# One decoder block with routed experts: routing, experts and combine joined in one block of programs

## What is computed

```python
logits = flat @ gate_W.T;  probs = softmax(logits)
top_v, top_i = top_k(probs, 2)                    # 8 experts, 2 for each token
out_e = (silu(x @ w1_e[e]) * (x @ w3_e[e])) @ w2_e[e]      # 128 -> 512 -> 128
routed = sum of top_v * out_e over the token's 2 experts
shared = mean over 8 small shared experts of the same form # together 128 -> 512 -> 128
out = layernorm(x + 0.5 * shared + 0.5 * routed)
```

## Time and profile before

| | us |
|---|---|
| median of 3 runs | 851.56 (851.37 to 851.6) |
| the profiled execution | 843.65 |
| its span | 841.9 |
| TensorE matmul busy | 713.6 (85%) |
| VectorE, ScalarE, GpSimd busy | 487.4, 481.5, 461.6 |
| TensorE's clock, mean | 0.927 of full |

### The profile page before, as it was taken

One profiled execution on the slowest core, in us unless ns is written; L12 is line 12 of the kernel. 1 busy time (PEld: TensorE's weight loads), 2 busy tenths in 40 slices (PEclk: granted clock), 3 DMA queues, 4 the chain that ended last, 5 costly groups with the idle time before them and its releaser, 6 DMA issues.

```text
span 841.9 us, 16996 instructions
## 1 busy us (share of the span) xinstructions
PE 713.6 (85%) x5112; PEld 650.7 (77%) x5113; DVE 487.4 (58%) x1435; ACT 481.5 (57%) x1441; POOL 461.6 (55%) x471
## 2 busy tenths in 40 slices
PE   5789999874999996898888888989889888999950
PEld 3668888763788885898888888888889887898750
DVE  3798999864899753433434343334333434446896
ACT  5889999821399722544445344445444444544796
POOL 3378988852111155266766666666666666541322
PEclk9999999875999997899999999999999999999985
DMA  5457555523211232011111111111111112215573
GB/s 172 151 176 227 176 181 168 151 75 102 74 51 51 76 84 64 24 41 42 44 44 41 44 41 44 44 44 41 41 44 44 44 42 42 38 58 154 149 217 109
DMA packets 87238, 72.57 MB, mean 86 GB/s; under 512 B 10067, under 2 KB 72411, under 8 KB 87195
## 3 DMA queue, kind: packets, MB, share of 16 engines
q1 hardware_dynamic: 77808, 53.43, 21.5%
q0 software_dynamic: 9088, 18.63, 8.3%
q10 hardware_dynamic: 298, 0.01, 0.0%
HBM read 50.14 MB, written 21.89 MB: 86 GB/s over the span
## 4 chain that ended last, share of the span: by engine, by line
PE 46%; issue 7%; DVE 5%; ACT 2%; another core or an unknown queue 1%; DMA 1%; ACTq 0%; POOLq 0%; POOL 0%; SPq 0%; DVEq 0%
PE bank L1325 15%; PE bank L1293 9%; PE bank L1294 9%; PE bank L1295 9%; PE bank L1285 2%; DVE xg L1609 2%; DVE f_st L1626 1%; DVE z L1620 1%; DVE f_hT L1597 1%; ACT xg L1571 1%; DMA f_x2T<-x2T_cols 1%; PE bank L1513 0%; PE bank L1512 0%; PE bank L1511 0%
## 5 line engine op out<-in xcount | busy, mean ns | idle before, releaser
L1403 DVE TENSOR_TENSOR e_hT<-e_sg,bank 128x512 f32<-128x512 f32 x142 | 97.7, 688 | 258.5 <-PE bank L1295 109.4
L1266 POOL DMA_INDIRECT y_rows<-e_y,dst_tab x142 | 148.0, 1042 | 108.5 <-ACT e_y L1357 75.8
L1293 PE MATMUL bank<-e_x_hi,e_w_hi 128*128 128x256 f32 x568 | 179.0, 315 | 29.9 <-issue 27.0
L1294 PE MATMUL bank<-e_x_lo,e_w_hi 128*128 128x256 f32 x568 | 167.1, 294 | 8.6 <-issue 7.8
L1295 PE MATMUL bank<-e_x_hi,e_w_lo 128*128 128x256 f32 x568 | 166.9, 294 | 4.2 <-issue 4.0
L1258 POOL DMA_INDIRECT xg<-x_rows,src_tab x130 | 130.1, 1001 | 55.1 <-issue 36.0
L1351 ACT ACTIVATE e_sg<-bank 128x512 f32<-128x512 f32 x142 | 84.6, 596 | 116.7 <-PE bank L1295 76.0
L1325 PE MATMUL bank<-w,e_hT 128*128 x1136 | 142.7, 279 | 4.7 <-issue 4.4
L1293 PEld LDWEIGHTS bank<-e_x_hi,e_w_hi 128*128 128x128 f32 x568 | 114.0, 201 | 37.1 <-issue 32.7
L1325 PEld LDWEIGHTS bank<-w,e_hT 128*128 128x128 f32 x1136 | 136.5, 196 | 6.0 <-issue 5.7
L1295 PEld LDWEIGHTS bank<-e_x_hi,e_w_lo 128*128 128x128 f32 x568 | 114.3, 201 | 9.5 <-issue 9.2
(11 more groups left out here) (172 smaller groups left out, 1544.2 us busy)
## 6 DMA issues: line engine op xcount, KB each, us to landing
yk<-y_rows SPq DMA_DIRECT2D x16, 512.0 KB, 4.4
xT_in<-in_xT_dram SPq DMA_DIRECT2D x16, 256.0 KB, 3.3
x_res<-in_x_dram SPq DMA_DIRECT2D x16, 256.0 KB, 3.6
w_in<-in_L_ffn_w_e_dram SPq DMA_DIRECT2D x16, 256.0 KB, 3.0
c_in<-in_ctx_dram SPq DMA_DIRECT2D x16, 256.0 KB, 2.9
cT_in<-in_ctxT_dram SPq DMA_DIRECT2D x16, 256.0 KB, 3.2
x_rows<-x SPq DMA_DIRECT2D x16, 256.0 KB, 2.4
x2T_cols<-x2T SPq DMA_DIRECT2D x16, 256.0 KB, 2.7
```

The lines of the kernel that those rows point to most:

```text
L1266: nc.gpsimd.indirect_dma_start(y_rows, bass.IndirectOffsetOnAxis(dst_tab[:, n:n + 1], 0), y[b % R][:, t, :], None).then_inc(scattered[b % ...
L1293: nc.tensor.matmul(at, w_hi[r % 2][:, w], x_hi[r][:, :], start=True, stop=False)
L1294: nc.tensor.matmul(at, w_hi[r % 2][:, w], x_lo[r][:, :], start=False, stop=False)
L1403: nc.vector.tensor_tensor(hT[par][:, half * HC:(half + 1) * HC, :].rearrange("p c n -> p (c n)"), sg[half][:, :], bank[2 + half][:, :], AL ...
```

## The change

- Routing, experts and combine become one block. `routing` returns its five programs; the barrier between routing and experts is gone, and buffers that both used (`sg`, `hT`, x) are now shared, in `Common`.
- The tail of the slot table, `look_back`, is done in two chunks in items 30 and 31 instead of four in items 31 to 34. `w_at` is written at item 33, in `owners`, and signalled by `w_at_ok`; `shares` follows at items 34 and 35.
- EARLY_X is 12 instead of 8, so there are 16 buffers for rows; PRE is gone. GpSimd issues the gathers of 16 blocks one after the other, and those of later blocks from b = 8 on. The unrolled steps are 0 to 11.
- The copies of the first two blocks' weights and x, and their transposes, move from the start of `experts` into the last items of routing (`ahead`).
- LEAD is 8 instead of 6. SP no longer waits for the late rows; VectorE does, in combine.

```diff
-EARLY_X, RING, PRE = 8, 4, 6
+EARLY_X, RING = 12, 4
 # routing, sync
-            sp.wait_ge(late_ld, 16 * (NG - EARLY))
+        sp.wait_ge(x_lo_ok, EARLY)
 # routing, gpsimd
             pool.wait_ge(src_ok, 1)
-            for b in range(PRE):
-                ...
 # routing, vector
-        LOOK = C0 + NC + 1
+    LOOK = C0 + NC
+            if n == 0:
+                dve.wait_ge(oh_used, NC)
+                c_.link(nc.vector.tensor_copy(found, bank[6][:, 0:NBT]))
+                c_.link(nc.vector.tensor_scalar(found_i, found.bitcast(I32), 16, None, ALU.logical_shift_right))
+                c_.link(nc.vector.tensor_copy(place, found_i))
+                c_.link(nc.vector.tensor_scalar(place, place, float(-CODE_0), None, ALU.add))
+                c_.add(nc.vector.tensor_scalar(at_i, place, 0.0, None, ALU.max))
+                c_.add(nc.vector.scalar_tensor_tensor(moved, ...))
+                c_.wait()
+                c_.add(nc.vector.tensor_scalar(at_t, at_i, shift + 1, shift, ...))
+                c_.add(nc.vector.tensor_scalar(at_p, at_i, P - 1, None, ALU.bitwise_and))
+            if n == 1:
+                c_.add(nc.vector.tensor_tensor(dst_tab[:, :], place, moved, ALU.max))
+                c_.wait()
+                nc.vector.tensor_tensor(src_tab[:, :], at_t, at_p, ALU.add).then_inc(src_ok, 1)
+        for n in range(EARLY * FC):
+            ...
+            ahead(n - EARLY * FC)
 # experts, gpsimd
-        for b in range(PRE, EARLY_X + R):
+        for b in range(EARLY_X + R):
             gather(b)
 # experts, tensor
-        for b in range(2):
-            transpose_x(b, 0, b)
+        def ahead(n):
+            if n == -1:
+                pe.wait_ge(late.w_at_ok, 1)
+            if -3 <= n < -1:
+                transpose_x(n + 3, 0, n + 3)
 # experts, scalar (vector alike, with w_low and x_low)
-        for b in range(2):
-            w_high(b, b)
-            x_high(b, b)
+        def ahead(n):
+            if n == -4:
+                act.wait_ge(late.w_at_ok, 1)
+            if -4 <= n < -2:
+                w_high(n + 4, n + 4)
+            if -2 <= n:
+                x_high(n + 2, n + 2)
 # decoder, every engine alike
                 def _(pe):
-                    one.tensor(pe)
+                    ahead, run = one.tensor(pe)
+                    zero.tensor(pe, ahead)
+                    run()
                     two.tensor(pe)
 # combine
-    LEAD = 6
+    LEAD = 8
+        dve.wait_ge(rows_in, 16 * LATE)
```

More of the change, by code:

```diff
@@ L108 @@
     y_ok: object = None
+    rows_split: object = None
+    rows_in: object = None
 def over(ap, n):
@@ L204, in _ @@
                 def _(act):
-                    one.scalar(act)
+                    ahead, run = one.scalar(act)
+                    zero.scalar(act, ahead)
+                    run()
                     two.scalar(act)
@@ L209, in _ @@
                 def _(dve):
-                    one.vector(dve)
+                    ahead, run = one.vector(dve)
+                    zero.vector(dve, ahead)
+                    run()
                     two.vector(dve)
@@ new lines, in routing, with sb @@
+    common = m["common"]
+    def sb(name, shape, dt=F32):
+        return m["work"].enter_context(nc.sbuf_tensor(name, shape, dt))
+    NK = NT * K
+    OC, C0 = 6, 2 * FC
+    NC = -(-NK // OC)
+    LOOK = C0 + NC
+    assert LOOK + 6 <= EARLY * FC
+    pick = [sb(f"pick{k}", [P, NT, E]) for k in range(K)]
+    pos = [sb(f"pos{n}", [P, NT, E]) for n in range(2)]
+    upto = sb("upto", [P, NT, E])
+    both = sb("both", [P, NT, E], BF16)
+    slot = sb("slot", [P, NT, K])
+    slot_i = sb("slot_i", [P, NK], I32)
@@ new lines, in routing @@
+    end = sb("end", [P, E])
+    start = sb("start", [P, E])
+    blk = sb("blk", [P, NK], BF16)
+    row = sb("row", [P, NK], BF16)
+    code = sb("code", [P, NK])
+    own = [sb(f"own{n}", [P, NB]) for n in range(2)]
+    found, place, moved = (pick[0][:, :, :].rearrange("p t e -> p (t e)")[:, n * NBT:(n + 1) * NBT] for n in range(3))
+    found_i, at_i = (pick[1][:, :, :].rearrange("p t e -> p (t e)")[:, n * NBT:(n + 1) * NBT].bitcast(I32)
+                     for n in range(2))
+    at_t, at_p = (pos[1][:, :, :].rearrange("p t e -> p (t e)")[:, n * NBT:(n + 1) * NBT].bitcast(I32)
+                  for n in range(2))
@@ L1329, in step @@
                 last.then_inc(y_ps, 1)
-        steps(pe, step)
+        return ahead, lambda: steps(pe, step)
     def scalar(act):
@@ L1380, in step @@
                 x_high(b + 2, (r + 2) % R)
-        steps(act, step)
+        return ahead, lambda: steps(act, step)
     def vector(dve):
@@ L1404, in hidden, with ahead @@
                                     sg[half][:, :], bank[2 + half][:, :], ALU.mult).then_inc(h_ok, 1)
-        for b in range(2):
-            w_low(b, b)
-            x_low(b, b)
+        def ahead(n):
+            if n == -4:
+                dve.wait_ge(late.w_at_ok, 1)
+            if -4 <= n < -2:
+                w_low(n + 4, n + 4)
+            if -2 <= n:
+                x_low(n + 2, n + 2)
         def late_low(i):
@@ L1428, in step @@
                 x_low(b + 2, (r + 2) % R)
-        steps(dve, step)
+        return ahead, lambda: steps(dve, step)
     return Programs(gpsimd=gpsimd, tensor=tensor, scalar=scalar, vector=vector, y_ok=y_ok)
```

555 lines of the change are left out of this document (255 added, 300 removed).

## The result

| | before | after |
|---|---|---|
| median of the runs made together | 851.46 us (4) | 859.5 us (4) |
| ratio, with its interval | | 1.0108 (1.007 to 1.0147) |
| profiled execution | 843.65 us | 856.62 us |
| its span | 841.9 us | 854.6 us |

The change makes the kernel slower, by 8.0 us in the medians and 12.7 us between the two profiled spans. Repeated in a later set of runs it came to the same ratio: 852.18 against 842.8 us, 1.0109. The profiled execution of before was a short one, 7.8 us under its median; that of after lies 2.9 us under its own. So the medians tell the size of the change better than the two spans do.

A forecast was written before the change was run, and what follows sets the result against it. It took unbroken runs of indirect DMAs to hold TensorE at 17 to 34% after some 7 us. Step 2 +6.2, early blocks -5.4, LEAD +3.0 gave +3.8: 847.4 in profile, 855.4 us median, range 836 to 862.

The forecast's parts named there:

- The offset of 7.9 us: Median of before (851.56) minus its profiled execution (843.65), added to the 847.4 us forecast for the profile.
- One block instead of two: Routing to experts: barrier and cold start removed; undisturbed, step 2's down-projection starts at 326.7, 18.7 us before 345.42.
- The slot table: End of routing: two chunks let the first gather start at 294.3 instead of 301.24, 6.9 us earlier.
- The gathers go on: GpSimd issues 32 gathers in one run of 39.8 us, to 334.1, without the earlier 5.75 us pause.
- The hold: TensorE beside the gather run: held 34.9 us at 34% pace, 23.0 us lost, plus 1.9 for slow clock.
- the second run of before: Second unbroken gather run before the change: TensorE's 1.44 us of work took 8.55 us, 17% pace.
- the mark: Start of step 2's down-projection, 345.42 before; forecast at 351.6, 6.2 us later.
- EARLY_X 12: Steps 9 to 12 of the experts run at 4.88 us instead of the disturbed pace: -5.4 us.
- LEAD 8: Combine: first gate product stands behind silu 8 instead of silu 6, +3.0 us in all, range 0 to 4.6.
- B: Rival: TensorE keeps the loop's pace in the long gather run; -14.0 us in all, 837.6; chance 28%.
- C: Rival: gathers cost TensorE nothing, the delay comes from the two removed blocks; -21.1 us, 830.5; chance 10%.

The follow-up runs named there:

- The kernel after with short pauses: The changed kernel with one GpSimd computation (0.78 us) after every third block of gathers: 771.44 us, ratio 0.9933, beside 777.48 for before.
- free chip: Chip, core and hour of the second or fourth set of runs, where the kernel before took 777.5 or 778.75 us.
- the long pauses: The changed kernel with two GpSimd computations (2.25 us pause) after every three blocks of gathers: 843.25 us, ratio 0.9917.
- holding chip: Chip, core and hour of the two other sets of runs, where the kernel before took 850.1 or 842.8 us.
- the run of 24: Gather run of the changed kernel with EARLY_X = 8 instead of 12, so 24 gathers instead of 32: 854.32 us, ratio 1.0041.
- the first set: Runs made together on one chip, where the kernel before took 850.1 us.
- the one with short pauses: The changed kernel with LEAD 6, blocks 0 to 11 gathered first with 0.78 us pauses, then scatters and gathers in turn: 837.64 us, ratio 0.9947.
- the third: Set of runs made together on another chip, where the kernel before took 842.8 us and the unchanged changed kernel 852.18.

## Why the prediction was right, point by point

The forecast was 855.4 us within 836 to 862, slower by 3.8; measured were 859.5 and 8.0. The sign and the mechanism held, the hold was priced too low, and the loop's part was missing. The prediction gave slower only 0.48 against 0.41 for faster, so the sign was close to a toss-up for it.

**The offset of 7.9 us between profile and median: luck.** The prediction took it from before, whose profiled execution was a short one, and added it to after, where it was 2.9 (859.5 - 856.62). In terms of profiles it said 847.4 and missed by 9.2 us; the median came within 4.1 because the offset was 5.0 us too large.

**One block instead of two, with no hold: step 2 at 326.7.** Close, 2.2 us too late. The kernel after with short pauses, on a free chip, has it at 324.54; with the long pauses on a holding chip it was 325.59. On a free chip before still starts step 2 at 333.97, with pauses that cost it nothing: there the barrier with what hangs on it, the later slot table among it, is worth 9.4 us. The rest of the way to 345.42 goes with the kind of chip.

**The slot table: first gather at 294.3.** Wrong by 2.7 us. `src_tab` was done at 292.2, 1.8 us ahead of the forecast, but GpSimd's low half of the last group of x stands ahead of the gathers in its program (295.50, 1.30 us) and waits for ScalarE's high half. The prediction looked at the release and not at what is queued ahead of the waiting instruction.

**The gathers go on: a run of 39.8 us.** Measured 40.7. The copies of `w_low` fall beside the gathers at 302.22 and 306.30, which took 1.28 and 1.43 us for 0.94: 0.34 and 0.49 us, where the prediction had 0.09 each. By the Trainium skill, SBUF — State Buffer, section on the two separate sides, GpSimd is locked out of writing descriptors while such a copy runs; as an estimate from that, up to 0.69 each, the copy's own time. The trace lies between: a part of the copy, not all of it. ScalarE's copy of `w_high` lies there too, and no run here parts the two.

**The hold: 34.9 us at 34% pace, 23.0 us lost, and 1.9 for the slow clock.** This is the term that was too small. From 7.2 us into the run to 2.3 us behind it are 35.8 us. TensorE lost 355.41 - 324.54 = 30.9 us; less the same 1.9 for the clock that is 29.0, or 19% pace: near the 17% of the second run of before, not the 34% of the first. The choice between the two ends was made by the kind of work, and that was no reason: the held work here is routing work too. The end of the hold was off as well: TensorE issues single matmuls until 342.48, 4.8 us behind the run (3.9 behind the run of 24), not 2.3. So 6.0 us more were lost than forecast; with the 2.2 us by which the start of the sum was too late, the mark comes **at +10.0 instead of +6.2**. The clock was at 1.2 GHz for much of it (0.69 over 34 us, 0.50 over the 9 after). Inside the hold that is part of the 19%; behind it TensorE worked at 1.2 GHz for some 3 us more, from 342.69, so the 1.9 us were enough.

**EARLY_X 12: -5.4.** Measured -5.45; all ten steps took 4.88 us.

**LEAD 8: +3.0.** The first gate product stands 33.8 us behind step 67 instead of 29.2: the +4.6 of the prediction. At the end of the span +2.1 are left, and taking LEAD back gave some 2.4 us in medians.

**Missing: the loop, +6.1 us in the one pair of profiles.** Its length differs between sets for one and the same kernel: after it is 342.80 us in one profile and 338.77 in the other (743.07 - 404.30). The kernel with LEAD 6 took 343.5 in the first set, the one with short pauses 337.7 in the third. By medians 1.3 to 2.7 us are left for it when 4.6 up to step 12 and 2.1 behind step 67 are taken off. Before has only one profile on a holding chip, 336.71, and that of a short execution. Whether the change has any part in this stays open.

**The rivals.** B (TensorE keeps the loop's pace in a long run) falls: 19% against 45% from which it decides. C (gathers cost nothing) falls on holding chips, since pauses alone bring 16 us, and is a fair description of the free ones. Beside C stood what the Trainium skill states in DMA: Bandwidth & Descriptors, section SWDGE vs HWDGE vs iDMA: a DMA engine goes round its queues in turn. Nothing here speaks against that. The DMA engines were busy for 0.21 of the held stretch, plain loads at the same rate held nothing, and TensorE came back without a new instruction packet; what holds TensorE isn't shown to be a DMA queue. The range was wide enough for the chips that hold, but it took no account of a chip of the other kind; before itself took 73 us less there.

## What to carry to other kernels

Idle time of TensorE with the releaser "issue", beside GpSimd that issues one indirect DMA after another, is a reason to break up the run. Here 2.25 us of computing between groups of six gathers did it. Bringing a long run of gathers forward to where TensorE is the bound can cost more than the barrier that it removes. And measure on more than one chip before tuning against such an effect: pauses of 2.25 us gained 16 us for the kernel after on one kind and nothing for the kernel before on the other, and a computation behind every step of a loop that GpSimd bounds cost 3%.

## What the runs showed of the hardware

- **Chips differ.** The same program took 850 and 843 us on two chips and 777 and 779 us on two others. On the first two, indirect DMAs back to back bring TensorE down to some 19% of its pace after 7 to 8 us; on the others it is busy for 189.45 of 200 us in a loop where GpSimd issues 151 of them without a break. What differs physically, and what the hold is, no run here shows; nor does any show a chip of one kind twice.
- **A dose.** From the first gather to step 2, where nothing is held: 27.5 us. With groups of six gathers (7.5 us) and 2.25 us of computing: 28.7. With 0.78 us, 24 gathers: 44.9. Without a pause: 49.0 for 24 gathers, 58.4 for 32.
- **It goes with the indirect DMA.** GpSimd computing without a break for 11.8 us, with 55 GB/s of plain loads beside it, left TensorE busy for 9.16 of 10 us. That rests on one execution.
